# Windowed attention on Trainium2: scores computed a second time, transposed, in place of transposing the probabilities on TensorE

## What is computed

```python
scores = jnp.einsum('bqhd,bkhd->bhqk', q, k) * scale
mask = (q_idx >= k_idx) & (q_idx - k_idx <= WINDOW - 1)   # WINDOW = 1024
scores = jnp.where(mask, scores, -inf)
probs = jax.nn.softmax(scores, axis=-1)
o = jnp.einsum('bhqk,bkhd->bqhd', probs, v)
```

## Time and profile before

| | us |
|---|---|
| median of the runs | 3633.87 |
| the two runs | 3618.48, 3649.27 |
| profiled execution, its own time | 3659.54 |
| its span, slowest core (core 4) | 3657.6 |
| spans of the 8 cores | 3589.9 to 3657.6 |

### The profile page before, as it was taken

How to read it: one execution, slowest core, us unless ns; L and a number is a source line. 1 busy time by engine, 2 the same in 40 slices (tenths; PEclk the granted TensorE clock), 3 DMA queues, 4 the chain that set the end, 5 groups by cost and what they waited for, 6 DMA issues and landing times. The chain is left out here.

```text
span 3657.6 us, 30112 instructions; the slowest of 8 cores (3589.9 to 3657.6 us)
## 1 busy us (share of the span) xinstructions
PE 1577.3 (43%) x7168; PEld 735.9 (20%) x7168; DVE 870.3 (24%) x2260; ACT 911.4 (25%) x1872; POOL 90.4 (2%) x153
## 2 busy tenths in 40 slices
PE   1226774124561477744444443443444363413333
PEld 0112331011220123222222222222222121101111
DVE  1110000452104200003232232322323212232222
ACT  4541115311023100113232232322323200232221
POOL 0000000000000000010000000000000000000000
PEclk9998887556775677775555555555555576656666
DMA  3212110001310222120000000000000234004443
GB/s 105 77 63 63 58 41 0 0 1 52 92 40 0 61 68 69 62 69 1 6 1 6 6 1 6 1 6 6 1 6 1 61 92 111 13 15 119 111 123 93
DMA packets 72840, 156.21 MB, mean 43 GB/s; under 512 B 12992, under 2 KB 12992, under 8 KB 70368
## 3 DMA queue, kind: packets, MB, share of 16 engines
q1 hardware_dynamic: 62016, 120.61, 11.9%
q0 software_dynamic: 10656, 33.67, 3.1%
HBM read 137.47 MB, written 16.78 MB: 42 GB/s over the span
## 5 line engine op out<-in xcount | busy, mean ns | idle before, releaser
L428 PE MATMUL psA<-wchunk,R 128*128 128x512 bf16 x1280 | 349.6, 433 | 283.9 <-DVE wchunk L411 283.9
L663 PE MATMUL psC<-identb,PTb 128*128 128x128 bf16 x640 | 169.4, 265 | 412.0 <-ACT PTb L669 375.6
L264 PE MATMUL psD<-identb,ropeo 128*128 128x128 bf16 x320 | 84.3, 263 | 537.8 <-DVE ropeo L512 263.6
L428 PE MATMUL psB<-wchunk,R 128*128 128x512 bf16 x1280 | 315.3, 403 | 0.0
L669 ACT COPY PTb<-psC 128x128 bf16<-128x128 bf16 x640 | 170.3, 266 | 308.1 <-PE psC L663 283.6
L428 PEld LDWEIGHTS psA<-wchunk,R 128*128 128x128 bf16 x1280 | 135.6, 107 | 481.4 <-issue 399.7
L663 PE MATMUL psD<-identb,PTb 128*128 128x128 bf16 x512 | 141.8, 277 | 151.4 <-DVE PTb L673 150.5
L271 ACT COPY R<-psD 128x128 bf16<-128x128 bf16 x384 | 102.1, 266 | 351.9 <-PE psC L264 276.3
L411 DVE CAST wchunk<-wstgA 128x512 bf16<-128x512 f32 x96 | 41.0, 427 | 612.8 <-PE psB L428 453.8
L673 DVE COPY PTb<-psD 128x128 bf16<-128x128 bf16 x512 | 115.2, 225 | 251.4 <-PE psC L663 191.1
L663 PEld LDWEIGHTS psC<-identb,PTb 128*128 128x128 bf16 x640 | 66.7, 104 | 526.7 <-issue 514.8
(11 more groups left out here) (105 smaller groups left out, 1888.7 us busy)
## 6 DMA issues: line engine op xcount, KB each, us to landing
wstgA<-wqkv SPq DMA_DIRECT2D x96, 256.0 KB, 2.7
wstgB<-wqkv SPq DMA_DIRECT2D x96, 256.0 KB, 2.8
wchunk<-x_all SPq DMA_DIRECT2D x16, 1024.0 KB, 4.8
vhbm<-PTb POOLq DMA_DIRECT2D x64, 128.0 KB, 2.1
R<-vhbm POOLq DMA_DIRECT2D x16, 512.0 KB, 6.0
wstgA<-wo SPq DMA_DIRECT2D x32, 256.0 KB, 3.2
wstgB<-wo SPq DMA_DIRECT2D x32, 256.0 KB, 3.4
R<-x_all POOLq DMA_DIRECT2D x32, 256.0 KB, 3.4
```

The costliest lines, as they stand in the source:

```text
L264: tv = pl.op("tensor", lambda e, s=slot, x=src_ap: e.transpose(s, x, identb[:]), sem=ct)
L428: ctm = pl.op("tensor", lambda e, d=d, t=t, ps=ps: e.matmul(ps, xlnT[:, lhs_col(t, d):lhs_col(t, d) + 128], wchunk[:, 512 * d:512 * (d + 1 ...
L663: tv = p.op("tensor", lambda e, s=slot, PT=PT, l=l: e.transpose(s, PT[:, 128 * l:128 * (l + 1)], identb[:]), sem=ct)
```

## The change

The attention stage of a tile now has two passes. The first computes for all 16 heads the scores with queries on the partitions and their negative row maxima (L603 and L607 of the new file). The maxima are cast to bf16 (L611, L613), transposed into rows in two rounds of eight (L627) and copied by ACT into `wstgA` and `wstgB` (L631). The second pass computes for each head and each of the 9 blocks the scores again with the keys on the partitions (L651), and adds the negative maximum of each query by a matmul of a row of ones with that row (L656), whose contraction is over one partition. ACT computes exp without a bias (L664) straight into the layout that PV needs. The transposes of `PT` and their 9 copies are gone. The masks are stored in the transposed layout. PE's wait for the ring now stands after the first pass; DVE's wait for the ring's DMA stands ahead of it.

Beside this, the compiler option's patch and an unused constant (101.0) are dropped, and `TrPipe.do` is written differently for the same instructions.

```diff
-import concourse.bass_utils as _bu
-        argv = ["--enable-ldw-opt=true" if a == "--enable-ldw-opt=false" else a
-                for a in argv]
...
+        red = {}
+        for h in range(NH):
...
+            for (off, n) in ((0, 512), (512, 512), (1024, 128)):
...
+            red[h] = p.op("vector", lambda e, ps=ps, h=h: e.tensor_reduce(
...
+            bank_guard[par] = (cv, red[h])
...
+        castb = p.op("vector", lambda e: e.tensor_copy(out=nmaxsb[:, 8:16],
+                                                       in_=nmaxs[:, 8:16]),
...
+        p.wait("tensor", cv, castb)
+        for b in range(2):
...
+            for h in range(8 * b, 8 * b + 8):
+                tv = p.op("tensor", lambda e, h=h, b=b: e.transpose(
+                    psDb[0:1, 128 * (h - 8 * b):128 * (h - 8 * b + 1)],
+                    nmaxsb[:, h:h + 1], identb[:]), sem=(ct if h == 8 * b + 7 else None))
+            p.wait("scalar", ct, tv)
+            nm[b] = p.op("scalar", lambda e, b=b: e.copy(
+                nmrow_half[b][0:1, 0:1024], psDb[0:1, 0:1024]),
...
         p.wait("tensor", cv, ring_ld[j + 8])
...
+            for l in range(NKT):
+                p.op("tensor", lambda e, ps=ps, l=l, kb=kbase, q=q_ap: e.matmul(
+                    ps[:, 128 * l:128 * (l + 1)],
+                    kT[:, kb + 128 * l:kb + 128 * (l + 1)],
+                    q, start=True, stop=False))
+                nmr = nmrow_half[h // 8][0:1, 128 * (h % 8):128 * (h % 8 + 1)]
+                ctst = p.op("tensor", lambda e, ps=ps, l=l, r=nmr: e.matmul(
+                    ps[:, 128 * l:128 * (l + 1)], ones[:], r, start=False, stop=True),
...
-        def emit_TR(h):
...
-                tv = p.op("tensor", lambda e, s=slot, PT=PT, l=l: e.transpose(
...
-        emit_S(0)
+        emit_ST(0)
         for h in range(1, NH):
-            emit_S(h)
-            emit_TR(h - 1)
+            emit_ST(h)
             emit_PV(h - 1)
-        emit_TR(NH - 1)
         emit_PV(NH - 1)
```

More of the change, by code:

```diff
@@ L4 @@
 import concourse.mybir as mybir
-import concourse.bass_utils as _bu
 from concourse.bass_utils import run_bass_kernel_spmd
-if not getattr(_bu, "_ldw_patch", False):
-    _orig_run_command = _bu.run_command
-    def _patched_run_command(argv, **kw):
-        argv = ["--enable-ldw-opt=true" if a == "--enable-ldw-opt=false" else a
-                for a in argv]
-        return _orig_run_command(argv, **kw)
-    _bu.run_command = _patched_run_command
-    _bu._ldw_patch = True
 F32 = mybir.dt.float32
@@ L38 @@
 CONSTS = [CPC, LN_EPS, RMS_EPS, 1.0 / 16.0, 128.0 * RMS_EPS, -0.2, 0.2,
-          0.5, 1.0, 0.0, 0.33, -0.33, 101.0]
+          0.5, 1.0, 0.0, 0.33, -0.33]
 class Ctr:
@@ L168, in build_nc @@
     m8 = (i_np[None, :] >= i_np[:, None]).astype(bfdt)
-    m0q = (i_np[:, None] < i_np[None, :]).astype(bfdt)
-    m8q = (i_np[:, None] >= i_np[None, :]).astype(bfdt)
-    masks_dram = nc.inline_tensor(np.concatenate([m0q, m8q], axis=1), name="masks_c")
+    masks_dram = nc.inline_tensor(np.concatenate([m0, m8], axis=1), name="masks_c")
     ident_dram = nc.inline_tensor(np.eye(128, dtype=bfdt), name="ident_c")
@@ L256, in do @@
             si = self.idx % 2
-            eng = "scalar" if self.idx % 2 == 0 else "vector"
-            ctr = cs if eng == "scalar" else cv
+            eng = "scalar" if si == 0 else "vector"
+            ctr = cs if si == 0 else cv
             self.idx += 1
@@ L266, in do @@
             pl.wait(eng, ct, tv)
-            if scale is None and eng == "vector":
+            if scale is None and si == 0:
+                g = pl.op("scalar", lambda e, s=slot, dd=dst_ap: e.copy(dd, s),
+                          ins=[slot], out=dst_ap, sem=cs)
+            elif scale is None:
                 g = pl.op("vector", lambda e, s=slot, dd=dst_ap: e.tensor_copy(
                     out=dd, in_=s), ins=[slot], out=dst_ap, sem=cv)
-            elif scale is None:
-                g = pl.op("scalar", lambda e, s=slot, dd=dst_ap: e.copy(dd, s),
-                          ins=[slot], out=dst_ap, sem=cs)
-            else:
[L274 to L278, removed]
+            elif si == 0:
+                g = pl.op("scalar", lambda e, s=slot, dd=dst_ap, sc=scale: e.activation(
+                    out=dd, in_=s, func=AF.Copy, scale=sc), ins=[slot], out=dst_ap, sem=cs)
+            else:
+                g = pl.op("vector", lambda e, s=slot, dd=dst_ap, sc=scale:
+                          e.tensor_scalar_mul(dd, s, sc), ins=[slot], out=dst_ap, sem=cv)
             self.guard[si] = (ctr, g)
@@ L589, in ring_validcol @@
                           ins=[vb], out=vdst, sem=cv)
[L591 to L594, removed]
     ldv0 = None
@@ L608, in build_nc @@
         if j >= 1:
+            sl = (j + 8) % NKT
             p.wait("gpsimd", ct, ring_guard[j - 1])
-            ring_load(j + 8)
+            ldv = ring_dma(j + 8)
+            p.wait("vector", RNG, ldv)
+            ring_validcol(j + 8)
+        red = {}
+        for h in range(NH):
+            par = h % 2
+            ps = (psA if par == 0 else psB)
+            if bank_guard[par] is not None:
+                c, v = bank_guard[par]
+                p.wait("tensor", c, v)
+            q_ap = qT[:, 1024 * h + 128 * j:1024 * h + 128 * (j + 1)]
+            ctm = None
+            for (off, n) in ((0, 512), (512, 512), (1024, 128)):
+                kbase = 2048 * h + 128 * j
+                ctm = p.op("tensor", lambda e, ps=ps, q=q_ap, kb=kbase, o=off, n=n: e.matmul(
+                    ps[:, o:o + n], q, kT[:, kb + o:kb + o + n], start=True, stop=True),
+                    sem=(ct if off == 1024 else None))
+            p.wait("vector", ct, ctm)
+            red[h] = p.op("vector", lambda e, ps=ps, h=h: e.tensor_reduce(
+                out=nmaxs[:, h:h + 1], in_=ps[:, 0:1152], axis=AX.X, op=ALU.max,
+                negate=True), ins=[ps[:, 0:1152]], out=nmaxs[:, h:h + 1], sem=cv)
+            bank_guard[par] = (cv, red[h])
@@ new lines, in build_nc @@
+        p.op("vector", lambda e: e.tensor_copy(out=nmaxsb[:, 0:8], in_=nmaxs[:, 0:8]),
+             ins=[nmaxs[:, 0:8]], out=nmaxsb[:, 0:8])
+        castb = p.op("vector", lambda e: e.tensor_copy(out=nmaxsb[:, 8:16],
+                                                       in_=nmaxs[:, 8:16]),
+                     ins=[nmaxs[:, 8:16]], out=nmaxsb[:, 8:16], sem=cv)
+        p.wait("tensor", cv, castb)
+        nm = {}
+        for b in range(2):
+            if b == 1:
+                p.wait("tensor", cs, nm[0])
+            elif j >= 1:
+                p.wait("tensor", cs, nm2_prev)
+                if psc_guard[1] is not None:
+                    p.wait("tensor", cs, psc_guard[1])
+            tv = None
+            for h in range(8 * b, 8 * b + 8):
[5 more added lines that the diff above has]
+                nmrow_half[b][0:1, 0:1024], psDb[0:1, 0:1024]),
+                ins=[psDb[0:1, 0:1024]], out=nmrow_half[b][0:1, 0:1024], sem=cs)
@@ L611, in build_nc, with emit_ST @@
+        nm2 = nm[1]
+        nm2_prev = nm2
         p.wait("tensor", cv, ring_ld[j + 8])
         mk_of = {}
-        ev_last = {}
-        def emit_S(h):
+        def emit_ST(h):
             par = h % 2
@@ L618, in emit_S @@
             if bank_guard[par] is not None:
-                for c, v in bank_guard[par]:
-                    p.wait("tensor", c, v)
-            q_ap = qT[:, 1024 * h + 128 * j:1024 * h + 128 * (j + 1)]
[L622 to L632, removed]
+                c, v = bank_guard[par]
+                p.wait("tensor", c, v)
+            if h == 0:
+                p.wait("tensor", cs, nm2)
+            kbase = 2048 * h + 128 * j
+            q_ap = qT[:, 1024 * h + 128 * j:1024 * h + 128 * (j + 1)]
+            ctst = None
+            for l in range(NKT):
[6 more added lines that the diff above has]
+                    ps[:, 128 * l:128 * (l + 1)], ones[:], r, start=False, stop=True),
+                    sem=(ct if l == NKT - 1 else None))
             PT = PTb[:, 1152 * par:1152 * (par + 1)]
-            p.wait("scalar", cv, red)
+            p.wait("scalar", ct, ctst)
             if pt_guard[par] is not None:
@@ L637, in emit_S @@
                 p.wait("scalar", c, v)
[L638 to L641, removed]
+            expv = p.op("scalar", lambda e, ps=ps, PT=PT: e.activation(
+                out=PT, in_=ps[:, 0:1152], func=AF.Exp), ins=[ps[:, 0:1152]], out=PT,
+                sem=cs)
+            bank_guard[par] = (cs, expv)
             p.wait("vector", cs, expv)
@@ L680, in emit_PV @@
             PT = PTb[:, 1152 * par:1152 * (par + 1)]
-            for c, v in ev_last[h]:
-                p.wait("tensor", c, v)
+            p.wait("tensor", cv, mk_of[h])
             if psc_guard[par] is not None:
@@ L713, in build_nc @@
     p.run("P5attn")
+    if kphases < 6:
+        return _finish_early()
     p = Plan(nc, OWN)
```

2 lines of the change are left out of this document (removed).

## The result

| | us |
|---|---|
| before, median of 10 runs | 3632.93 |
| after, median of 11 runs | 3309.45 (3299.80 to 3360.09) |
| ratio after to before | 0.9126 [0.9086, 0.9167] |
| profiled execution of after, its own time | 3313.47 |
| its span, slowest core (core 0) | 3311.7 |

A forecast was written before the change was run, and what follows sets the result against it. The attention stage was taken as bound by a chain of PE, DVE and ACT taking turns. Replacing its 1208.5 us by 646 gave 3659.5 - 1208.5 + 646 = 3097, less 25.7 is 3071, stated as 3070, range 3020 to 3215.

The forecast's parts named there:

- The chain through the transposes: Attention stage before: PE, DVE and ACT take turns over PT's transposes and copies, 8.89 us a head, 1138 for 128.
- The first pass: Attention stage, per tile: 16 maxima on DVE at 1.46 us each with the scores hidden, 23.4 us.
- the second rival: First pass: scores do not hide behind the other bank's reduce, 44.5 us instead of 23.4, 3239 in all; chance 5%.
- The turn: Between a tile's two passes: casts, two rounds of eight transposes and ACT copies, all added waits; 5.3 us.
- The reload: Ring reload between tiles, from the last PV's end to the validity copy's end: stays at 6.5 us.
- The edits priced at nothing: Dropped compiler flag, unused constant, masks in transposed layout and rewritten transpose helper: no cost.
- the third rival: Every matmul: without the compiler flag no weight load runs beside a matmul; 3953 in all, slower; chance 3%.
- the second pass: Attention stage, per tile: PE binds with 27 matmuls at 0.107, 2.89 us a head, 48.3 us at 1.2 GHz; 44.2 at 2.4.
- the middle, 646: Attention stage total taken between 665 us at 1.2 GHz and 626 us at 2.4 GHz, expecting the clock to rise.
- The first rival: Rank-1 matmuls: their weight load is exposed, 0.141 us more each, 163 us in all, 3253; chance 10%.
- the loop of 2.77 us: Second pass, ACT and DVE: exp, two masks, reciprocal and scaling with gaps, 2.77 us a head, binding at 2.4 GHz.
- the 25.7 that were taken off for the median: Whole kernel: the profiled run of before stood 25.7 us above its median of 3633.9, so 3097 became 3071.

The follow-up runs named there:

- the run without the option: The kernel before with only the compiler option's patch taken out, nothing else changed: 3612.7 us in one run.
- the grouped kernel: The changed kernel with each head's nine score matmuls issued first and its nine one-row rank-1 matmuls after them: 3086.83 us in one run.

## Why the prediction was wrong, step by step

What held. The chain through the transposes was the bound, and removing it removed its waits. The first pass came at 23.3 to 23.6 us (forecast 23.4): the scores hide behind the maxima, so the second rival is out. The turn took 5.4 in all tiles but the first (forecast 5.3; the copy of 1024 columns 1.00, priced 1.10). The reload stayed, 6.4 to 6.9 (6.5). The edits priced at nothing cost nothing that shows, and the third rival is out by the run without the option.

What failed is one term, the second pass: 79.5 us where the forecast had 48.3 at 1.2 GHz. That is 31.2 a tile, 250 us over eight tiles, and takes the 665 us of the stage at 1.2 GHz to 915; 916.5 were measured (1602.38 to 2518.92). Two statements stand behind it:

- "I take 0.107, since it has a PV's columns and the PV rows are the nearest." The columns were right, and the rows were the wrong neighbours: in every row of before a 128-row load follows a 128-row matmul. At a change of height the next matmul comes late, and that twice, on the rank-1 matmul and on the full-height matmul behind it. 18 matmuls a head cost 0.2165 - 0.107 = 0.109 more each, 1.97 us, or 31.5 a tile.
- "The second pass at 1.2 GHz leaves PE no idle time, so I expect the clock to rise in it." PE had no idle time and the clock stayed at 0.50. That is why the middle, 646, was too low even before the first error, by 19 us. Hidden loads would not by themselves have mended this: the grouped kernel had PE busy 49.0 of 50 us and stayed at 0.50 too.

The first rival was the right kind of event ("the weights change height at every matmul") and was given 10% and 3253. It counted one loss of the two: 9 x 0.141 = 1.27 a head where 18 x 0.109 = 1.97 were paid. Counted twice and at the load's 98 ns, it would have been 18 x 0.098 x 128 = 226 us over 3090, 3316. The argument held against it, that loads are hidden everywhere in the trace, was drawn from a trace that has no change of height.

The Trainium skill ("TensorE: Matmul & The Clock Gate", Part 3, The mechanism) has loads overlap with running matmuls only where their row groups differ. The runs don't bear that out: loads of 128 rows behind 128 rows, or of one row behind one row, use the same rows and overlap (0.107 from start to start), while one row or 64 beside 128 don't (0.2165 and 0.22). The same section lets a load into the background weight buffer go ahead too, of which these rows show nothing. A load into rows that the running matmul doesn't use at all occurs in no run here. The prediction was right to put the rule aside for PV, and wrong to price the rank-1 matmul as if it didn't matter which rows are in use.

A smaller term was off too, and shows only where PE doesn't bind: the loop of 2.77 us is 2.34. The exp without a bias takes 1.13 (1.22 with one), and the gaps of 0.10 that I put between neighbours on one engine belong to instructions that wait for the one ahead. One that doesn't starts before the other's record ends: the reciprocal 0.09 before the end of the mask (1762.53 against 1762.62), the exp 0.11 before the end of the scaling (1763.11 against 1763.22).

The rest of the difference has the other sign. 916.5 - 646 = 270 us too little in the stage, but 3309 - 3070 = 239 in all. The other 31 us lie outside of the stage. There the profiled execution of before took 2451 us (3659.5 - 1208.5) and that of after 2397 (3313.5 - 916.5), 54 less, and the 25.7 that were taken off for the median stand for about half of that. Of the 54, 30 lie ahead of the stage: the profile of before was of core 4, whose V projection ended late (last load of L428 at 1590.6; in after on core 0 at 1560.2, and on core 0 of before at 1559.5), at a granted clock of 0.75 from 1240 to 1602 where core 0 of the same execution had 0.82. These 30 us the change neither made nor removed. The remaining 24 lie behind the stage and were not followed.

## What to carry to other kernels

Between matmuls that follow each other closely keep the stationary operands equally high: a rank-1 update interleaved with full matmuls doubled the price of both (0.107 to 0.2165 us, at 1.2 GHz), and operands padded with zeros to 128 rows, or the short matmuls grouped, took the run from 3309 to 2989 us, with the clock's part in it, and to 3087. A duration read from a trace is good for the neighbours it had there; where a change makes new neighbours, price the pair. And once the big wait is gone, look at the order on the small engines: a reciprocal that stood behind masks it doesn't need was worth 0.3 us a head.
